# A graph network on one Trainium2 core: in the stage of attention sums, the two halves of a pair of edge blocks take turns head by head on two column halves and two row groups of the PE array

## The reference, cut to what matters

```python
# layer 0: attention with H = 4 heads
xw    = (x @ W).reshape(n, H, C)
alpha = leaky_relu(a_src[src] + a_dst[dst] + a_edge)
attn  = segment_softmax(alpha, dst)
agg   = segment_sum(xw[src] * attn[:, :, None], dst)
proj  = (agg.reshape(n, H * C) + bias) @ Wp + bp
h     = x + elu(proj)
x1    = layernorm(x + layernorm(h) * gamma + beta)
# layer 1: point transformer
d     = gelu(layer_norm(gelu(layer_norm(ea3 @ Wd1 + bd1)) @ Wd2 + bd2))
a     = segment_softmax((x1 @ W1)[dst] - (x1 @ W2)[src] + d, dst)
out   = layernorm(x1 + segment_sum(a * ((x1 @ W3)[src] + d), dst))
```

## Time and profile before

| | |
|---|---|
| device time, 3 runs | 2307.57 us median, 2290.02 to 2311.89 |
| span of the profiled execution | 2281.3 us |
| PE / PEld / DVE busy over the span | 1697.7 / 925.5 / 1608.6 us |
| ACT / POOL busy | 704.6 / 1071.7 us |
| stage of attention sums | about 965 to 1500 us of the span |

### The profile page before, as it was taken

How to read it: one execution, slowest core, us unless ns; L and a number is a source line. 1 busy time by engine, 2 the same in 40 slices (tenths; PEclk the granted TensorE clock), 3 DMA queues, 4 the chain that set the end, 5 groups by cost and what they waited for, 6 DMA issues and landing times. The chain is left out here.

```text
span 2281.3 us, 29583 instructions
## 1 busy us (share of the span) xinstructions
PE 1697.7 (74%) x6749; PEld 925.5 (41%) x6749; DVE 1608.6 (71%) x4249; ACT 704.6 (31%) x1168; POOL 1071.7 (47%) x1254
## 2 busy tenths in 40 slices
PE   6888798888878880099999999358676766667673
PEld 4555565555555540023333333247433333333331
DVE  2667676676767678657666766448598887878786
ACT  2545454454555440012222222025311111111111
POOL 3555554455555440002434444610267676667764
PEclk9999898999999985579778988668799888889886
DMA  2333333343334341101111111100112111112120
GB/s 69 102 110 123 108 120 109 103 125 108 120 113 126 107 115 35 27 11 25 37 33 36 39 35 31 35 5 3 30 43 47 42 46 41 46 44 50 43 49 14
DMA packets 154993, 142.83 MB, mean 63 GB/s; under 512 B 83688, under 2 KB 103103, under 8 KB 154948
## 3 DMA queue, kind: packets, MB, share of 16 engines
q1 hardware_dynamic: 122948, 112.22, 16.2%
q0 software_dynamic: 32000, 30.10, 6.7%
HBM read 71.30 MB, written 73.65 MB: 64 GB/s over the span
## 5 line engine op out<-in xcount | busy, mean ns | idle before, releaser
L415 POOL DMA_INDIRECT dense_pairs<-in_x_dram,dense_stage x400 | 411.1, 1028 | 128.1 <-issue 127.8
L1011 PE MATMUL bank<-first_zb,Mstack 128*64 128x512 f32 x400 | 246.0, 713 | 2.7 <-DVE first_zb L1091 2.2
L1452 POOL DMA_INDIRECT out_dram<-second_orow,second_stage x200 | 199.5, 997 | 85.1 <-issue 62.0
L1444 POOL DMA_INDIRECT second_pairs<-x_table,second_stage x200 | 209.3, 1047 | 61.6 <-issue 55.3
L967 POOL DMA_INDIRECT x_table<-first_xr,first_stage x200 | 198.2, 991 | 61.4 <-issue 60.7
L1091 DVE TENSOR_TENSOR first_zb<-bank,XT 128x512 f32<-128x512 f32 x200 | 135.2, 688 | 88.3 <-PE bank L1004 57.7
L961 POOL COPY first_stage<-first_rows 128x4 int32 (+1 forms) x50 | 10.1, 203 | 384.5 <-DVE first_xr L1160 259.5
L450 PE MATMUL bank<-dense_xT,Mblk 128*128 128x512 f32 x196 | 117.4, 684 | 63.2 <-ACT dense_xT L520 60.2
L455 PE MATMUL bank<-dense_hb,prm 128*128 128x512 f32 x196 | 128.4, 742 | 47.5 <-DVE dense_hb L580 43.2
L477 PEld LDWEIGHTS bank<-prm,dense_xT 128*128 128x128 f32 x784 | 122.1, 222 | 59.8 <-issue 59.8
L585 DVE TENSOR_SCALAR dense_v<-bank 128x8 f32<-128x8 f32 x98 | 16.0, 163 | 166.5 <-remote 132.7
(11 more groups left out here) (267 smaller groups left out, 3885.7 us busy)
## 6 DMA issues: line engine op xcount, KB each, us to landing
dense_rows<-in_x_dram SPq DMA_DIRECT2D x98, 256.0 KB
x_table<-dense_xr SPq DMA_DIRECT2D x98, 256.0 KB
out_dram<-dense_orow SPq DMA_DIRECT2D x98, 256.0 KB
dense_pairs<-in_x_dram,dense_stage POOLq DMA_INDIRECT x400
target_rows<-first_xr SPq DMA_DIRECT2D x50, 128.0 KB
second_pairs<-target_rows SPq DMA_DIRECT2D x50, 128.0 KB
second_mask<-mask_rows SPq DMA_DIRECT2D x50, 128.0 KB
first_mask<-mask_rows SPq DMA_DIRECT2D x50, 64.0 KB
```

The costliest lines, as they stand in the source:

```text
L415: pool.indirect_dma_start(out=pairs[a][:, j % 4, F * (j // 4):F * (j // 4) + F], out_offset=None, in_=x, in_offset=bass.IndirectOffsetOnAx ...
L1011: nc.tensor.matmul(pY[64 * s:64 * s + 64, :], Mstack[:, h, :], zb[(n - 2) % 4][:, :], start=(h == 0), stop=(h == H - 1)).then_inc(z_used, 1)
L1444: pool.indirect_dma_start(out=pairs[u.off % 2][:, j, 0:F], out_offset=None, in_=x1, in_offset=bass.IndirectOffsetOnAxis(ap=stage[a][:, j:j ...
L1452: pool.indirect_dma_start(out=out, out_offset=bass.IndirectOffsetOnAxis(ap=stage[a][:, 4 + j:5 + j], axis=0), in_=orow[a][:, j, :], in_off ...
```

## The change

- The two halves alternate: step n is head n // 2 of half 1 - n % 2. Neighbouring head sums thus write the two column halves of the array (partitions 64 to 127 and 0 to 63 of the result).
- `wt` has 56 partitions of 512 columns: half 0 on partitions 0 to 23, half 1 on 32 to 55; `headsel` is held twice in the same way. Neighbouring spreads read different rows of the array and write different PSUM banks.
- TensorE's slot is `centre`, then groups of two spreads followed by two head sums of the head before, with `variance` before the first two of them that follow spreads 4 and 5, and two `to_rows` behind each of the last two groups. `centre` works on pair u-2, not u-1.
- `pY` is two banks, and both scans of a pair are made in the next slot, after products 1 and 3. `elu`, `residual` and the parts on ScalarE go with them to later places.
- The weights of a pair come with two DMAs, so a pair's load has four.

```diff
-        headsel = sb("headsel", [24, H, 128], bf16)
+        headsel = sb("headsel", [56, H, 128], bf16)
...
-                nc.vector.tensor_copy(headsel[:, :, :], c128("head")[0:24, :].rearrange("r (h m) -> r h m", h=H))
+                for s in range(2):
+                    nc.vector.tensor_copy(headsel[32 * s:32 * s + 24, :, :],
+                                          c128("head")[0:24, :].rearrange("r (h m) -> r h m", h=H))
...
-            wt = [sbp(f"wt{i}", [24, 2 * COLS], bf16) for i in range(2)]
+            wt = [sbp(f"wt{i}", [56, COLS], bf16) for i in range(2)]
...
-            pB, pY, pH, pR, pG = [bank[0], bank[1]], bank[2], bank[4], bank[5], bank[6]
+            pB, pY, pH, pR, pG = [bank[0], bank[1]], [bank[2], bank[3]], bank[4], bank[5], bank[6]
...
-                    sp.dma_start(wt[b][:, :], weight_rows[:, bass.ds(u.count(0) * (-2 * COLS) + (PAIRS - 1) * 2 * COLS, 2 * COLS)])\
-                        .then_inc(w_loaded[b], 16)
                     for s in range(2):
+                        sp.dma_start(wt[b][32 * s:32 * s + 24, :], weight_rows[:, columns(u, s)]).then_inc(w_loaded[b], 16)
                         sp.dma_start(mask[b][64 * s:64 * s + 64, :],
...
+                def spread(u, n):
+                    b, s, h = u.off % 2, 1 - n % 2, n // 2
                     if n == 0:
+                        pe.wait_ge(w_loaded[b], u.halves(1) * 64)
+                    atleast(pe, z_made, u.count(0) * (2 * H) + (n - 1))
+                    nc.tensor.matmul(pB[n % 2][:, :], headsel[32 * s:32 * s + 24, h, :], wt[b][32 * s:32 * s + 24, :],
+                                     start=True, stop=True).then_inc(spread_made, 1)
+
+                def head_sum(u, n):
+                    b, s, h = u.off % 2, 1 - n % 2, n // 2
+                    if h == 0:
+                        atleast(pe, halfway if s else summed, u.count(-1))
+                    pe.wait_ge(z_made, u.count(0) * (2 * H) + (n + 1))
+                    nc.tensor.matmul(pY[b][64 * s:64 * s + 64, :], Mstack[:, h, :], zb[n % 4][:, :],
+                                     start=(h == 0), stop=(h == H - 1)).then_inc(z_used, 1)
...
                 def slot(u):
+                    if u.back(2).valid(PAIRS):
+                        centre(u.back(2))
+                    for h in range(H + 1):
+                        if u.valid(PAIRS) and h < H:
+                            spread(u, 2 * h)
+                            spread(u, 2 * h + 1)
+                        if h == 2 and u.back(2).valid(PAIRS):
                             variance(u.back(2))
+                        if u.valid(PAIRS) and h > 0:
+                            head_sum(u, 2 * h - 2)
+                            head_sum(u, 2 * h - 1)
+                        if h > 2 and u.back(2).valid(PAIRS):
+                            to_rows(u.back(2), 2 * h - 6)
+                            to_rows(u.back(2), 2 * h - 5)
...
                 def slot(u):
-                    if u.back(1).valid(PAIRS):
-                        elu_parts(u.back(1))
                     if u.back(3).valid(PAIRS):
                         square_y(u.back(3))
-                    if u.valid(PAIRS):
-                        copy_targets(u)
+                    if u.back(2).valid(PAIRS):
+                        square(u.back(2))
                     if u.back(1).valid(PAIRS):
-                        square(u.back(1))
+                        copy_targets(u.back(1))
+                        elu_parts(u.back(1))
...
-                    nc.vector.tensor_tensor(zb[n % 4][:, :], pB[n % 2][:, :], XT[:, columns(u, 1 - n // H)], ALU.mult)\
+                    nc.vector.tensor_tensor(zb[n % 4][:, :], pB[n % 2][:, :], XT[:, columns(u, 1 - n % 2)], ALU.mult)\
...
-                    dve.wait_ge(z_used, u.count(0) * (2 * H) + (2 - s) * H)
+                    dve.wait_ge(z_used, u.count(1) * (2 * H))
...
                     for n in range(2 * H):
                         if u.valid(PAIRS):
                             product(u, n)
...
+                        if n in (1, 3) and u.back(1).valid(PAIRS):
+                            scan(u.back(1), 1 if n == 1 else 0)
+                            cross(u.back(1), 1 if n == 1 else 0)
+                        if n == 3 and u.back(3).valid(PAIRS):
+                            sum_squares(u.back(3))
+                        if n == 5:
+                            if u.back(4).valid(PAIRS):
+                                finish(u.back(4))
                             if u.back(2).valid(PAIRS):
                                 add_eps(u.back(2))
...
+                        if n >= 5 and has_roots:
+                            root(u.back(2), 2 * n - 9)
+                            root(u.back(2), 2 * n - 8)
+                    if u.back(1).valid(PAIRS):
+                        elu(u.back(1))
+                    if has_roots:
+                        root(u.back(2), 7)
+                    if u.back(1).valid(PAIRS):
+                        residual(u.back(1))
+                    if has_roots:
+                        root(u.back(2), 8)
                     if u.back(2).valid(PAIRS):
                         scale(u.back(2))
                     if u.back(3).valid(PAIRS):
                         flag(u.back(3))
-                    if u.valid(PAIRS):
-                        scan(u, 0)
                     if u.back(2).valid(PAIRS):
                         add_scaled(u.back(2))
-                    if u.valid(PAIRS):
-                        cross(u, 0)
```

More of the change, by code:

```diff
@@ L994, in _ @@
             def _(pe):
-                def sums(u, n):
-                    b = u.off % 2
+                def spread(u, n):
+                    b, s, h = u.off % 2, 1 - n % 2, n // 2
                     if n == 0:
[L1000 to L1012, removed]
+                        pe.wait_ge(w_loaded[b], u.halves(1) * 64)
[9 more added lines that the diff above has]
+                                     start=(h == 0), stop=(h == H - 1)).then_inc(z_used, 1)
                 def centre(u):
@@ L1034, in slot @@
                 def slot(u):
-                    for n in range(2 * H + 2):
-                        if u.valid(PAIRS):
-                            sums(u, n)
-                        if n == 0 and u.back(2).valid(PAIRS):
-                            variance(u.back(2))
[L1040 to L1043, removed]
+                    if u.back(2).valid(PAIRS):
[5 more added lines that the diff above has]
+                        if h == 2 and u.back(2).valid(PAIRS):
+                            variance(u.back(2))
+                        if u.valid(PAIRS) and h > 0:
[4 more added lines that the diff above has]
+                            to_rows(u.back(2), 2 * h - 5)
                 slots(pe, PAIRS, 5, slot)
@@ L1095, in scan @@
                     b, half = u.off % 2, slice(64 * s, 64 * s + 64)
-                    dve.wait_ge(z_used, u.count(0) * (2 * H) + (2 - s) * H)
+                    dve.wait_ge(z_used, u.count(1) * (2 * H))
                     atleast(dve, e_made, u.count(-1))
                     atleast(dve, crossed, u.count(0) * 2 + (1 - s))
-                    nc.vector.tensor_tensor_scan(ys[b][half, ::-1], mask[b][half, ::-1], pY[half, ::-1], start[half, :],
+                    nc.vector.tensor_tensor_scan(ys[b][half, ::-1], mask[b][half, ::-1], pY[b][half, ::-1], start[half, :],
                                                  ALU.mult, ALU.add).then_inc(halfway if s else summed, 1)
@@ L1180, in slot @@
                             product(u, n)
-                        if n == 1 and u.back(1).valid(PAIRS):
-                            elu(u.back(1))
-                        if n == 2 and u.back(1).valid(PAIRS):
-                            residual(u.back(1))
-                        if n == 3:
-                            if u.back(3).valid(PAIRS):
-                                sum_squares(u.back(3))
+                        if n in (1, 3) and u.back(1).valid(PAIRS):
[6 more added lines that the diff above has]
+                                finish(u.back(4))
                             if u.back(2).valid(PAIRS):
                                 add_eps(u.back(2))
-                        if n == 4 and u.valid(PAIRS):
-                            scan(u, 1)
-                        if n == 5 and u.back(4).valid(PAIRS):
-                            finish(u.back(4))
-                        if n >= 4 and has_roots:
-                            root(u.back(2), 2 * n - 7)
-                        if n == 4 and u.valid(PAIRS):
-                            cross(u, 1)
-                        if n >= 4 and has_roots:
-                            root(u.back(2), 2 * n - 6)
+                        if n >= 5 and has_roots:
[9 more added lines that the diff above has]
+                        root(u.back(2), 8)
                     if u.back(2).valid(PAIRS):
```

## The result

The changed kernel takes 2209.38 us (median of 4 runs, 2186.68 to 2225.23) against 2302.17 for the kernel before on the same chip: ratio 0.9582, with a 95% interval of 0.9504 to 0.9659. The profiled execution has a span of 2207.6 us at a mean clock of 0.827 (before: 2281.3 at 0.843).

A forecast was written before the change was run, and what follows sets the result against it. TensorE was taken as the bound in the attention sums, with VectorE waiting. Mean slot 18.6 to 16.3 us, 2.3 us x 24 slots = 55 us, other edits about nothing: 2307.6 - 55 = 2252 us, range 2212 to 2318.

The forecast's parts named there:

- I take a middle value from the order of the passes: TensorE, two neighbouring head sums: only two of four passes lie beside each other, 1.43 us between bounds 1.00 and 1.86.
- All overlaps: Rival, TensorE's head sums: overlap is full, VectorE's 13.6 us bind, mean slot 14.9, gain 88 us, 2219 us; chance 0.12.
- Mean with the same clock: Attention-sum slot: clock stays 0.84, so 14.5 us at full and 22.3 at lower clock average 16.3 us.
- The clock rival: Attention-sum stage: TensorE's waits drop the clock to 0.60, slot 20.1 us, 36 us slower, 2344 us; chance 0.11.
- the prediction's own model: Attention-sum slot: full-clock and lower-clock lengths weighted by time share; before, 16.2 and 27.1 give 18.6 us against 18.9 measured.
- (a): TensorE's order: spreads and head sums in twos pay 0.10 and 0.15 us of going over four times, not eight and six.
- nothing overlaps: Rival, TensorE's slot: only fewer changes of form help, 15.3 us at full clock, gain 20 us, 2288 us; chance 0.25.
- Filling and emptying: Start and end of the attention-sum stage: first slot 3 us shorter, emptying about as much longer, 0, at most 5 us.
- The gain is a difference and carries over: Whole kernel: the 55 us gain, summed against the profiled 2281.3 us span, applies to the runs: 2307.6 to 2252 us.
- VectorE's 13.6 us: Attention-sum slot at the full clock: VectorE alone needs 13.6 us, its instructions unchanged.
- `scale` late next: VectorE at the slot's end: `scale` waits for the last `to_rows`, starting at 13.1, not 12.25; waits of 0.9 us.
- The share of time at the lower clock: Attention-sum stage: clock 0.84 means 32% of the time at the lower level, 0.60 means 80%.

The follow-up runs named there:

- single turns: Changed kernel, but one spread and one head sum in turn: 0.9580 of the kernel before (1899.93 us); with one half first as well, 0.9676 (1923.35 us).
- the mixed order: Changed kernel, but head sums 0 to 3 singly, 4 with 5 and 6 with 7 together: 0.9496 of the kernel before (1890.03 us), 0.9533 on a slower chip.
- 13 matmuls more: Changed kernel plus unread matmuls in each slot, 7 ahead of spread 2 and 6 ahead of spread 4: 0.9637 of the kernel before, 1915.58 us.

## Why the prediction was wrong, and where it was right

- **The step that failed** is "I take a middle value from the order of the passes ... three passes, 1.28 + 0.15 = 1.43 us". Measured: 1.00 at the full clock, 1.90 at the lower, for two head sums. The argument was that A1 A2 B1 B2 go in order, so that only A2 and B1 can lie beside each other. It was wrong in this: two passes, one of each half, start together (both within the first 0.09 us), so the half that comes second doesn't wait until both passes of the first are through. "All overlaps", to which I gave 0.12, was the case. With the overlap taken away the same four passes took 1.87.
- **"Mean with the same clock"** failed too, in the other direction: 0.84 became 0.71, below the 0.75 that it had named as a sign of being wrong. The clock rival had the direction and "TensorE now waits in several places"; it decided from 0.68 downward with the forecast's prices. Put into the prediction's own model, the two errors give the measured slot: 1 / (0.42/13.6 + 0.58/18.9) = 16.2 us, measured 16.0. With the clock at 0.84 the model gives 14.9; by this model the lower clock took back 1.1 x 24 = 26 us. That the forecast slot of 16.3 came so near to the measured 16.0 is luck: the two errors nearly cancelled.
- **(a), the order in twos as a saving** of 0.10 and 0.15 us each time, failed as well: without overlap in either, twos have slots of 17.09 us and single turns 15.28, on two quick chips, and nothing in the sum stood for this cost. The rival "nothing overlaps" was priced at 20 us of gain with the clock unchanged; in single turns it gained 67 us (1923 against 1990), since its slots are the rival's 15.3 of the full clock and the clock stayed at 0.99.
- **Filling and emptying "0, at most 5 us either way"**: filling 0.9 longer, emptying 13.3 shorter. Another execution of the kernel before emptied in 57.3, so 8 to 13 us belong to the change; which part of it does this was not tried.
- **"The gain is a difference and carries over"**: the profiled executions differ by 73.7 us, the medians by 92.8. The profiled execution of before was a quick one: in every later run a time lies only 2 to 4 us above its span, so that its 2281.3 stands below the 2290 to 2312 of the timed runs. The one of after stood at its median (span 2207.6, median 2209.4). The miss of 43 us adds up: 5.4 is the other median of before, 19.1 is this, and 18.5 are slots 69.5 - 55.2 = 14.3 (half of it because the model took 18.6 for the 18.9 of before), emptying and filling 12.4, less 8.2 in the rest of the program. The overlap and the clock together make only the other half of the 14.3, 7 us: what took the time out of the range was mostly not the mechanism.
- **Right**: TensorE was the bound; the waits before products and scans went (144 to 25 us); VectorE's 13.6 us (the quickest steady slots of the mixed order, 13.6 to 13.8); the price of nothing overlapping (15.3, measured 15.4); the load in time (no wait for a DMA but the first); `scale` late next. Its 2.2 us against 0.9 go with the lower clock, where the `to_rows` and head sums ahead of it take almost twice as long (two head sums 1.90 us against 1.00; with 13 matmuls more, at 0.92, the wait is 1.4).
- **The share of time at the lower clock**, 0.32 at a mean of 0.84 and 0.80 at 0.60 in the prediction's sums, rests on how far the two levels lie apart. No run shows them as frequencies; what the traces show is a granted clock of 0.50 or 1.00 (kernel before, 150 stretches of 1 us from 965 to 1115 us: 50 at 0.50, 91 at 1.00, 9 between). From 0.50 the share at 0.84 is 0.16 / 0.50 = 0.32, so this term of the sum stands.

What stays open: at which idle pattern the clock falls, and which of the parts that moved with the scans gives the gain. The waits of 1.00 and 0.21 us stand ahead of its fall in the slot shown, single turns with one wait of about 1 us kept 0.99 on one chip and 0.92 on another, and that is all that the runs say.

## What to carry to other kernels

Two matmuls on the two column halves of the array cost one (1.00 us for 1.87 here), so put them together where a result behind them is waited for: 0.85 us saved there shortened the slot by 0.87. Elsewhere the saved time can turn into idle TensorE and cost its clock, as it did here in the order in twos (0.71, with 13 matmuls more 0.92, in single turns 0.99, all on the quick chips): after such a change read the granted clock of the stage before the busy times. A gain can have two sources in one edit; here the moved scans, with what moved beside them, gave 3% on one chip with no overlap at all, and the order that uses the overlap only at the slot's end was ahead of both.

## What was not expected of the hardware

- fp32 head sums of two passes each overlap fully by column halves: 1.00 us for two against 1.87 without, 1.90 at the lower clock. Two bf16 spreads on different row groups take 0.54 us at the lower clock against 0.96 on the same rows, and the slot, 16.69 us on the same rows, was 1.0 us shorter on different ones.
- The same program takes 1928 us on one chip and 2209 to 2270 on others, mostly ahead of this stage: its first residual stands at 791 us in one and at 995 to 1046 in the others. Single turns, 1% ahead of the changed kernel by their ratio on the quick kind, were level with it on the slow one.
- In the changed kernel on the slower chips TensorE stands up to 3.0 and 3.7 us before a spread with nothing in the trace that ends the wait; on the quick one none of its waits in the steady part is longer than 1.1 us, all are ended by a product, and its slots repeat to 0.1 us in a pattern of three (16.1, 16.5, 15.2).
